# The first sum of a Laplacian stencil, computed by GpSimd instead of DVE, in a fused attention and convolution kernel

## The chip, the cores and the metric

One core of a Trainium2 chip runs the whole program. The metric is the time of one execution on the device in microseconds (us); several executions are timed, and the median counts. The engines are TensorE (PE, with its weight loads PEld), DVE (VectorE), ACT (ScalarE), POOL (GpSimd) and SP, which issues all DMAs here. They run in parallel, each through its own list of instructions, and meet at semaphores.

## The reference

The input x has the shape (8, 192, 128, 128), in float32. Two layers follow one another, each added to its input, each on a group-normalised input (`_gn`, 32 groups).

```python
x = x + _L0_conv_ref(_gn(x), ...)
x = x + _L1_conv_ref(_gn(x), merge_w, merge_b)
```

The first layer is attention within windows of 8x8 pixels with 6 heads of 32 channels. Queries and keys are multiplied in the frequency domain, the result meets the values, a position bias is added, then come softmax, the product with the values and a projection. The second layer is a Laplacian and a 1x1 convolution:

```python
lap = jnp.array([[0.0, -1.0, 0.0], [-1.0, 4.0, -1.0], [0.0, -1.0, 0.0]])
edges = lax.conv_general_dilated(x, lap_k, ..., feature_group_count=c)
out = x + edges
y = lax.conv_general_dilated(out, merge_w, window_strides=(1, 1), padding='VALID', ...)
```

So the second layer needs, for each pixel, five times itself minus its four neighbours: that is the stencil.

## The kernel before, in words

The work of the first layer is cut into 1024 pairs of windows (`PAIRS`), 128 per image. The kernel is one hand-written software pipeline: every engine runs the same loop over iterations `it`, and `pair(lag)` gives the pair whose step with that lag is due, so that six or so pairs are in flight. Eight iterations are a block (`blk, ph = divmod(it, 8)`), one strip of 8 image rows; 16 blocks are an image, and c is a block's number within its image. The second layer follows 17 blocks behind for the stencil (`STENCIL_LAG`) and 18 for the merge matmuls (`MERGE_LAG`). The order of work on each engine is the order in which the code of one iteration is written. Attention spans blocks 0 to 127, the stencil blocks 17 to 144, so blocks 17 to 127 have both.

One iteration, as far as the steps of the prediction touch it:

- TensorE transposes the probabilities (L418), runs one merge piece of the second layer (L394 to L401, phases 0 to 5), computes queries, keys and values (L456), transposes v (L460), projects (L472 to L475), multiplies probabilities and values (L485), transforms back (L495), transforms forward (L505), and forms the scores (L525).
- DVE adds the bias to the scores (L712), takes their maxima (L717), multiplies in the frequency domain (L721), finishes a merge piece (`result`, L697), runs the stencil and statistics steps that are due, splits q and k (`qkl`, L800, which L505 needs), adds the projection to x (L808), sums the exponentials (L818), splits part of x (L822), takes statistics (L705) and takes reciprocals (L851).
- GpSimd normalises the probabilities of one pair (L936, behind the reciprocal), splits x every fourth iteration (`xl`, L942, phases 2 and 6), and subtracts the maxima of a newer pair (L947, behind the maximum).
- ScalarE does the exponential (L904, behind L947) and then the copy `qkh` (called at L908, all copies are recorded at L859), which L800 needs.

The stencil of a strip has three units (channels 0 to 127 in two halves of four rows, and the 64 others). For each unit DVE runs three instructions:

- `diagonal` (L658): dg = the pixel rows below, shifted left, plus the rows above, shifted right; 5 rows of 129 elements from the tiles `src_a` or `src_b` (all parts of the tensor `late`);
- `neighbours` (L666): two shifted parts of dg are added, which gives the sum of the four neighbours;
- `stencil` (L674): 5 times the pixel minus that sum; phase 6 of the last unit lets the merge matmuls of the next block start.

`diagonal` is due in phases 0, 2 and 4, `neighbours` in 1, 3 and 5, `stencil` in 2, 4 and 6. dg has two buffers that the units use in turn. The first unit waits for the borders of the tile (`border_w`, written by DVE in phase 7) and for its load (`src_in`).

Other DVE steps stand behind the stencil in some blocks: the statistics of the next image's input (`stat_read`, L558, in phases 0, 1, 6 and 7 for c below 12, not in the last image); at c = 12 their aggregation (L564, phase 0); at c = 13 the scaled weights of the next image (L587 to L597, phases 2 to 4); at c = 1 the scaled merge weights (L794, phase 2).

Of the kernel before, what the change touches and what calls it, by code (L numbers as in the profile page):

```python
# [9 lines left out]
ALU = mybir.AluOpType  # L10
# [18 lines left out]
STENCIL_LAG, MERGE_LAG = 17, 18  # L29
# [61 lines left out]
def program(nc, x, out, w):  # L91
    B, _, H, W = x.shape
# [4 lines left out]
    PAIRS, STRIPS = B * NP, B * NS  # L97
# [7 lines left out]
    with ExitStack() as ctx:  # L105
        def sb(name, shape, dtype=F32):
            return ctx.enter_context(nc.sbuf_tensor(name, shape, dtype))
# [4 lines left out]
        def sem(name):  # L112
            return ctx.enter_context(nc.semaphore(name))
# [28 lines left out]
        dg = sb("dg", [128, 2, 5 * (W + 1)])  # L142
# [3 lines left out]
        src_a = [late[:, k * SA:(k + 1) * SA].rearrange("p (r c) -> p r c", c=PW) for k in range(3)]  # L146
        at = 3 * SA
        src_b = [late[:, at + k * SB:at + (k + 1) * SB].rearrange("p (r c) -> p r c", c=PW) for k in range(3)]
        at += 3 * SB
        za = late[:, at:at + 2048].rearrange("p (k n) -> p k n", k=2)  # L150
        zb = late[:, at + 2048:at + 3072].rearrange("p (k n) -> p k n", k=2)
# [21 lines left out]
        src_in = [sem(f"src_in{k}") for k in range(3)]  # L173
# [15 lines left out]
        border_w, diag_done, nb_done, z_done = map(sem, ("border_w", "diag_done", "nb_done", "z_done"))  # L189
# [39 lines left out]
        def pairs():  # L229

            def counted(i):
                return (i, i + 1) if 0 <= i < PAIRS else None
            for it in iterations:
                yield it, lambda lag, it=it: counted(it - lag)
# [11 lines left out]
        def tokens(o, t, h, up=0):  # L246
            lo = up
            return o[lo:lo + (CA if t == 0 else CB), h % 2, :].rearrange("p (w r c) -> p w r c", w=8, c=WS)

        block = ctx.enter_context(nc.Block())  # L250

# [279 lines left out]
        def _(dve):  # L531
            V = nc.vector
# [113 lines left out]
            def scored(i):  # L646
                return probs[:, i % 3, :, :]

            units = ((src_a, 0, za, 0), (src_b, 0, zb, 0), (src_a, 4, za, 512))

            def diagonal(v, unit):

                if unit == 0:
                    dve.wait_ge(border_w, v + 1)
                    dve.wait_ge(src_in[v % 3], 48 * (v // 3 + 1))
                src, r, _, _ = units[unit]
                s = src[v % 3]
                V.tensor_tensor(dg[:, unit % 2, :].rearrange("p (r c) -> p r c", c=W + 1),  # L658
                                s[:, r + 1:r + 6, 0:W + 1], s[:, r:r + 5, 1:W + 2], ALU.add).then_inc(diag_done, 1)

            def neighbours(v, unit):

                _, _, z, at = units[unit]
# [43 lines left out]
            for it, pair in pairs():  # L707
                blk, ph = divmod(it, 8)
# [18 lines left out]
                if task:  # L727
                    kind, at, p = task
# [24 lines left out]

                v = blk - STENCIL_LAG
                if 0 <= v < STRIPS:
                    if ph == 0:
                        diagonal(v, 0)
                    elif ph == 1:
                        neighbours(v, 0)
                    elif ph == 2:  # L760
                        stencil(v, 0)
                        diagonal(v, 1)
                    elif ph == 3:
                        neighbours(v, 1)
                    elif ph == 4:
                        stencil(v, 1)
                        diagonal(v, 2)
                    elif ph == 5:
                        neighbours(v, 2)
                    elif ph == 6:  # L770
                        stencil(v, 2)
                img, c = divmod(blk, NS)
# [72 lines left out]
                v = blk - STENCIL_LAG + 1  # L845
# [81 lines left out]
        @block.gpsimd  # L927
        def _(pool):
            P = nc.gpsimd
            P.memset(sm[:, :, :], 0.0)  # L930
            P.memset(ones[:, :], 1.0).then_inc(ones_done, 1)
            for it, pair in pairs():
                if pair(3):
                    i, n = pair(3)
                    pool.wait_ge(rec_done, n)
                    P.tensor_tensor(probs[:, i % 3, :, :], probs[:, i % 3, :, :],  # L936
                                    srec[:, i % 2, :].unsqueeze(2).broadcast_to([128, 6, N]),
                                    ALU.mult).then_inc(norm_done, 1)
                h = (it + 4) // 4
                if it % 4 == 2 and 0 <= h < PAIRS // 4:  # L940
                    pool.wait_ge(xh_done, 3 * h + 2)
                    P.tensor_tensor(tokens(xl, 0, h), windows(0, h), tokens(xh, 0, h).bitcast(F32), ALU.subtract  # L942
                                    ).then_inc(xl_done, 1)
                if pair(2):
                    i, n = pair(2)
                    pool.wait_ge(max_done, n)
                    P.tensor_tensor(probs[:, i % 3, :, :], probs[:, i % 3, :, :],  # L947
                                    smax[:, i % 2, :].unsqueeze(2).broadcast_to([128, 6, N]),
                                    ALU.subtract).then_inc(sub_done, 1)


# [28 lines left out]
```

## Time and profile before

| what | value |
|---|---|
| median of 3 runs | 6623.4 us (6617.2 to 6633.11) |
| profiled execution | 6616.41 us, span of its instructions 6614.6 us |
| TensorE busy | 6291.9 us (95%) |
| weight loads busy | 5340.6 us (81%) |
| DVE busy | 5312.2 us (80%), 11941 instructions |
| ScalarE busy | 3664.4 us (55%) |
| GpSimd busy | 2064.8 us (31%), 2310 instructions |
| mean granted clock of TensorE | 0.978 of full speed |

How to read it: busy time counts from the start to the end of each instruction; neighbouring instructions of one engine overlap a little, so a step in the chain can be shorter than the instruction itself. "Idle before" is the time in which an engine had nothing to do before an instruction, with the instruction that released it. The chain of work that ended last is followed back from the last instruction, at each step to what released it. Times in the trace are us from the start of the span.

### The profile page before, as it was taken

The page shows a single profiled execution, that of the slowest core. Times are in us where ns is not written, and L with a number is a line of the kernel's source. Part 1 is how long each engine was busy: PE and PEld are TensorE (multiplying, and loading weights), DVE is VectorE, ACT ScalarE, POOL GpSimd, SP SyncE. Part 2 cuts the span into 40 slices and gives each one's busy share as a digit, 9 for nine tenths or more (in the row PEclk, how much of TensorE's full clock was granted, in tenths as well). Part 3 has the DMA queues.
Part 4 walks back from the last instruction along what each step waited for, and adds up shares of the span by engine and source line. Part 5 has one row for each costly group of instructions (what it writes and reads, how often), then busy time and mean ns, then how long its engine had stood idle before and what let it go on. Part 6 is the DMA issues. An engine that isn't in the chain of part 4 may idle for free.

```text
span 6614.6 us, 222120 instructions
## 1 busy us (share of the span) xinstructions
PE 6291.9 (95%) x95620; PEld 5340.6 (81%) x95620; DVE 5312.2 (80%) x11941; ACT 3664.4 (55%) x9024; POOL 2064.8 (31%) x2310
## 2 busy tenths in 40 slices
PE   7999999999999999999999999999999999999976
PEld 5888788888888888888888888888888888888844
DVE  5777788888888888888888888888888888888854
ACT  3666655555555555555555555555555555555500
POOL 1333333333333333333333333333333333333300
PEclk9999999999999999999999999999999999999966
DMA  3221133232332322322333223323223222232233
GB/s 128 66 66 40 56 93 90 84 84 82 89 104 71 97 82 83 104 70 81 98 90 96 72 82 92 101 77 91 82 83 104 77 78 70 64 85 64 69 99 92
DMA packets 378995, 551.42 MB, mean 83 GB/s; under 512 B 23398, under 2 KB 283561, under 8 KB 365738
## 3 DMA queue, kind: packets, MB, share of 16 engines
q1 hardware_dynamic: 378028, 537.21, 28.5%
q8 instruction: 768, 12.58, 0.8%
q14 instruction: 199, 1.63, 0.1%
HBM read 335.80 MB, written 201.33 MB: 81 GB/s over the span
## 4 chain that ended last, share of the span: by engine, by line
PE 58%; DVE 25%; POOL 9%; ACT 6%; issue 2%; SPq 0%; DMA 0%; DVEq 0%; ACTq 0%
PE b_q L456 13%; PE b_t L505 7%; POOL probs L947 5%; PE b_s L525 5%; PE b_s L418 4%; DVE qkl L800 4%; DVE bn L705 4%; PE b_o L495 4%; PE b_o L394 3%; DVE late L808 3%; PE b_o L396 3%; ACT probs L904 3%; DVE ssum L818 3%; PE b_s L485 3%; POOL xl L942 3%; DVE probs L712 2%
## 5 line engine op out<-in xcount | busy, mean ns | idle before, releaser
L936 POOL TENSOR_TENSOR probs<-probs,srec 128x384 f32<-128x384 f32 x1024 | 849.3, 829 | 3723.1 <-DVE srec L851 3723.1
L800 DVE TENSOR_TENSOR qkl<-b_q,qkh 128x384 fp32r<-128x384 f32 x1024 | 567.6, 554 | 634.9 <-ACT qkh L859 628.3
L947 POOL TENSOR_TENSOR probs<-probs,smax 128x384 f32<-128x384 f32 x1024 | 908.0, 887 | 413.8 <-DVE smax L717 413.8
L712 DVE TENSOR_TENSOR probs<-b_s,posb 128x384 f32<-128x384 f32 x1024 | 553.0, 540 | 331.2 <-PE b_s L525 330.6
L904 ACT ACTIVATE probs<-probs 128x384 f32<-128x384 f32 x1024 | 535.3, 523 | 479.8 <-POOL probs L947 479.1
L456 PE MATMUL b_q<-wnh,xh 128*128 128x192 f32 (+1 forms) x2048 | 791.7, 387 | 3.1 <-DVE xhl L822 2.7
L859 ACT ACTIVATE probsT<-b_s 128x384 f32<-128x384 f32 x1024 | 502.4, 491 | 501.3 <-PE b_s L418 501.3
L859 ACT ACTIVATE qh<-b_t 94x384 f32<-94x384 f32 x1024 | 498.4, 487 | 480.4 <-PE b_t L505 480.4
L525 PEld LDWEIGHTS b_s<-vT,osb 32*64 32x64 f32 x24576 | 450.6, 132 | 284.5 <-ACT osb L859 204.9
L859 ACT ACTIVATE yT<-b_s 128x256 f32<-128x256 f32 x1024 | 392.7, 384 | 460.3 <-PE b_s L485 458.2
L456 PE MATMUL b_q<-wnl,xh 128*128 128x192 f32 (+1 forms) x2048 | 632.5, 309 | 0.0
L808 DVE SCALAR_TENSOR_TENSOR late<-b_s,pb,xs 128x128 f32<-128x128 f32 (+1 forms) x2048 | 610.1, 339 | 27.2 <-PE b_s L475 5.2
L456 PE MATMUL b_q<-wnl,xhl 128*128 128x192 f32 (+1 forms) x2048 | 631.0, 308 | 0.0
L456 PE MATMUL b_q<-wnh,xhb 128*128 128x192 f32 (+1 forms) x2048 | 630.5, 308 | 0.0
L456 PE MATMUL b_q<-wnh,xl 128*128 128x192 f32 (+1 forms) x2048 | 629.6, 307 | 0.0
L859 ACT ACTIVATE vs<-b_q 128x192 f32<-128x192 f32 x1024 | 334.9, 327 | 518.6 <-PE b_q L456 512.9
L717 DVE TENSOR_REDUCE smax<-probs 128x6 f32<-128x384 f32 x1024 | 566.5, 553 | 35.5
L525 PE MATMUL b_s<-vT,osb 32*64 32x64 f32 x24576 | 592.4, 225 | 0.9 <-DVE late L808 0.7
L505 PE MATMUL b_t<-qkh,fwdh 64*94 64x384 f32 x2048 | 423.1, 410 | 171.0 <-DVE qkl L800 170.7
L495 PE MATMUL b_o<-inv_sb,prod 94*64 94x64 f32 x12288 | 582.9, 230 | 0.0
L418 PE MATMUL b_s<-ident_sb,probs 128*128 128x128 f32 x3072 | 561.3, 292 | 1.2 <-ACT yT L859 1.2
L721 DVE TENSOR_TENSOR prod<-qh,b_t 94x384 f32<-94x384 f32 x1024 | 553.5, 541 | 1.9 <-ACT qh L859 1.9
(143 smaller groups left out, 15231.2 us busy)
## 6 DMA issues: line engine op xcount, KB each, us to landing
ld<-in_x SPq DMA_DIRECT2D x96, 1024.0 KB, 4.9
late<-x_dram SPq DMA_DIRECT2D x112, 640.0 KB, 6.3
xs<-in_x SPq DMA_DIRECT2D x128, 512.0 KB, 5.7
x_dram<-late SPq DMA_DIRECT2D x128, 512.0 KB, 2.8
out<-late SPq DMA_DIRECT2D x128, 512.0 KB, 4.6
late<-x_dram SPq DMA_DIRECT2D x240, 192.0 KB, 6.7
xs<-in_x SPq DMA_DIRECT2D x128, 256.0 KB, 6.3
x_dram<-late SPq DMA_DIRECT2D x128, 256.0 KB, 3.6
```

What stands on the lines that cost most here:

```text
L418: last = nc.tensor.transpose(b_p[:, t * 128:(t + 1) * 128], probs[:, i % 3, 2 * t:2 * t + 2, :].rearrange("p w m -> p (w m)"), ident[:, :])
L456: last = mm(o, xx[:, h % 2, at], ww[:, par, t, lo:up], start=(k == 0), stop=(k == 4))
L495: last = mm(b_o[g * N:(g + 1) * N, k * N:(k + 1) * N], prod[:, g * 3 + k, :, :].rearrange("p h d -> p (h d)"), inv[:, :], start=True, stop ...
L505: last = mm(b_t[0:NF, win * 512:win * 512 + QK], ff[rows, :], xx[rows, :], start=(k == 0), stop=(k == 2))
L525: last = mm(scores[h * N:(h + 1) * N, s * N:(s + 1) * N], osb[r:r + HD, k, :], vT[r:r + HD, i % 2, int(t > g), win * N:(win + 1) * N], sta ...
L712: V.tensor_tensor(scored(i).rearrange("p (t w) m -> p t w m", w=2), scores.rearrange("p (t w m) -> p t w m", w=2, m=N), posb[:, :, :].unsq ...
L800: V.tensor_tensor(qkl[:, :], q_out, qkh[:, :].bitcast(F32), ALU.subtract).then_inc(lo_out, 1)
L808: last = V.scalar_tensor_tensor(out=x1s[0:m, t, u % 2, :].rearrange("p (r c) -> p r c", c=W)[:, :, col:col + 16], in0=b_r[0:m, t * 128:(t ...
L859: return A.activation(o, i, ACT.Copy)
L904: A.activation(pr, pr, ACT.Exp).then_inc(exp_done, 1)
L936: P.tensor_tensor(probs[:, i % 3, :, :], probs[:, i % 3, :, :], srec[:, i % 2, :].unsqueeze(2).broadcast_to([128, 6, N]), ALU.mult).then_i ...
L947: P.tensor_tensor(probs[:, i % 3, :, :], probs[:, i % 3, :, :], smax[:, i % 2, :].unsqueeze(2).broadcast_to([128, 6, N]), ALU.subtract).th ...
```

## The change

`diagonal` goes from DVE's list to GpSimd's, at the end of GpSimd's iteration, behind the subtraction of the maxima, in the same phases 0, 2 and 4. On GpSimd it waits, beside the borders and the load, for `nb_done`, so that the dg buffer it writes has been read. The operands, the shape and the two buffers are the same. `neighbours` and `stencil` stay on DVE and wait for `diag_done` as before.

```diff
@@ -646,18 +648,6 @@
-            def diagonal(v, unit):
-
-                if unit == 0:
-                    dve.wait_ge(border_w, v + 1)
-                    dve.wait_ge(src_in[v % 3], 48 * (v // 3 + 1))
-                src, r, _, _ = units[unit]
-                s = src[v % 3]
-                V.tensor_tensor(dg[:, unit % 2, :].rearrange("p (r c) -> p r c", c=W + 1),
-                                s[:, r + 1:r + 6, 0:W + 1], s[:, r:r + 5, 1:W + 2], ALU.add).then_inc(diag_done, 1)
...
@@ -753,18 +743,14 @@
-                    if ph == 0:
-                        diagonal(v, 0)
-                    elif ph == 1:
+                    if ph == 1:
                         neighbours(v, 0)
                     elif ph == 2:
                         stencil(v, 0)
-                        diagonal(v, 1)
                     elif ph == 3:
                         neighbours(v, 1)
                     elif ph == 4:
                         stencil(v, 1)
-                        diagonal(v, 2)
...
@@ -929,7 +915,20 @@
+            def diagonal(v, unit):
+                if unit == 0:
+                    pool.wait_ge(border_w, v + 1)
+                    pool.wait_ge(src_in[v % 3], 48 * (v // 3 + 1))
+                if 3 * v + unit >= 2:
+                    pool.wait_ge(nb_done, 3 * v + unit - 1)
+                src, r, _, _ = units[unit]
+                s = src[v % 3]
+                P.tensor_tensor(dg[:, unit % 2, :].rearrange("p (r c) -> p r c", c=W + 1),
+                                s[:, r + 1:r + 6, 0:W + 1], s[:, r:r + 5, 1:W + 2], ALU.add).then_inc(diag_done, 1)
+
             for it, pair in pairs():
+                blk, ph = divmod(it, 8)
...
@@ -947,6 +946,9 @@
+                v = blk - STENCIL_LAG
+                if 0 <= v < STRIPS and ph in (0, 2, 4):
+                    diagonal(v, ph // 2)
```

DVE's list in phase 0 of an ordinary block, before (from the scores' bias to the split of q and k; the waits stand in brackets):

```order
L712 TENSOR_TENSOR probs<-b_s,posb 128x384 [waits s_mm]
L717 TENSOR_REDUCE smax<-probs 128x6 [waits s_out]
L721 TENSOR_TENSOR prod<-qh,b_t 94x2x3x64 [waits qh_out]
L697 SCALAR_TENSOR_TENSOR late<-b_o,mc,late 128x256 [waits out_sent0,m_mm]
L658 TENSOR_TENSOR dg<-late 128x645 [waits src_in0,border_w]
L558 BN_STATS bn<-ld 128x6 [waits ld_in1]
L800 TENSOR_TENSOR qkl<-b_q,qkh 128x384 [waits hi_out]
```

And the same place now (the changed file's lines are shifted: L702 is the old L712, L786 the old L800):

```order
L702 TENSOR_TENSOR probs<-b_s,posb 128x384 [waits s_mm]
L707 TENSOR_REDUCE smax<-probs 128x6 [waits s_out]
L711 TENSOR_TENSOR prod<-qh,b_t 94x2x3x64 [waits qh_out]
L687 SCALAR_TENSOR_TENSOR late<-b_o,mc,late 128x256 [waits out_sent0,m_mm]
L560 BN_STATS bn<-ld 128x6 [waits ld_in1]
L786 TENSOR_TENSOR qkl<-b_q,qkh 128x384 [waits hi_out]
```

The addition and its two waits are gone from between `result` and the statistics; nothing else has moved on DVE.

GpSimd's list before, over three iterations, the last of them with the split of x:

```order
L936 TENSOR_TENSOR probs<-probs,srec 128x384 [waits rec_done]
L947 TENSOR_TENSOR probs<-probs,smax 128x384 [waits max_done]
L936 TENSOR_TENSOR probs<-probs,srec 128x384 [waits rec_done]
L947 TENSOR_TENSOR probs<-probs,smax 128x384 [waits max_done]
L936 TENSOR_TENSOR probs<-probs,srec 128x384 [waits rec_done]
L942 TENSOR_TENSOR xl<-xs,xh 128x512 [waits xh_done]
L947 TENSOR_TENSOR probs<-probs,smax 128x384 [waits max_done]
```

And now, phases 0, 1 and 2 of a block (L935, L941 and L946 are the old L936, L942 and L947; the addition is listed under L927, the head of GpSimd's part):

```order
L935 TENSOR_TENSOR probs<-probs,srec 128x384 [waits rec_done]
L946 TENSOR_TENSOR probs<-probs,smax 128x384 [waits max_done]
L927 TENSOR_TENSOR dg<-late 128x645 [waits nb_done,src_in2,border_w]
L935 TENSOR_TENSOR probs<-probs,srec 128x384 [waits rec_done]
L946 TENSOR_TENSOR probs<-probs,smax 128x384 [waits max_done]
L935 TENSOR_TENSOR probs<-probs,srec 128x384 [waits rec_done]
L941 TENSOR_TENSOR xl<-xs,xh 128x512 [waits xh_done]
L946 TENSOR_TENSOR probs<-probs,smax 128x384 [waits max_done]
L927 TENSOR_TENSOR dg<-late 128x645 [waits nb_done]
```

The addition stands behind the subtraction and in front of the next iteration's normalisation, which waits for DVE's reciprocal.

## Rows read from the trace of the kernel before

**Rows 1.** The page: busy time of the engines; the chain that ended last, by engine

```profile
PE 6291.9 (95%) x95620; PEld 5340.6 (81%) x95620; DVE 5312.2 (80%) x11941; ACT 3664.4 (55%) x9024; POOL 2064.8 (31%) x2310
...
PE 58%; DVE 25%; POOL 9%; ACT 6%; issue 2%; SPq 0%; DMA 0%; DVEq 0%; ACTq 0%
```

**Rows 2.** Groups of instructions: names, shapes xcount | busy us, mean ns | idle before us

```profile
L936 POOL TENSOR_TENSOR probs<-probs,srec 128x384 f32<-128x384 f32 x1024 | 849.3, 829 | 3723.1 <-DVE srec L851 3723.1
...
L942 POOL TENSOR_TENSOR xl<-xs,xh 128x512 fp32r<-128x512 f32 x256 | 328.4, 1283 | 102.2 <-ACT xh L859 102.2
...
L658 DVE TENSOR_TENSOR dg<-late 128x645 f32<-128x645 f32 x384 | 315.8, 822 | 0.0
```

**Rows 3.** The chain in order of time, phases 5 to 0: start us, us, what

```profile
2657.38 0.60 DVE late L808 x2
...
2661.29 1.25 POOL probs L947
...
2675.66 0.76 PE b_t L505 x6
```

**Rows 4.** The chain, L658 in phase 0: first, second and last of 65

```profile
906.27 0.74 DVE dg L658
...
954.46 0.74 DVE dg L658
...
5276.56 0.74 DVE dg L658
```

**Rows 5.** Timeline, phase 0 of an ordinary block: start us, us, engine, instruction [idle before]

```profile
2674.32 0.47 ACT L859 ACTIVATE qkh<-b_q 128x384 fp32r<-128x384 f32 x1
2674.47 0.68 DVE L558 BATCH_NORM_STATS2 bn<-ld 128x6 f32<-128x512 f32 x1
...
2675.07 0.53 DVE L800 TENSOR_TENSOR qkl<-b_q,qkh 128x384 fp32r<-128x384 f32 x1
...
2675.66 0.41 PE L505 MATMUL b_t<-qkh,fwdh 64*94 64x384 f32 x2 [0.43 <-DVE qkl L800]
```

**Rows 6.** Timeline, phase 0 of a block of the last image

```profile
6011.23 0.56 DVE L800 TENSOR_TENSOR qkl<-b_q,qkh 128x384 fp32r<-128x384 f32 x1 [0.28 <-ACT qkh L859]
```

**Rows 7.** Timeline of TensorE: c = 12 in phase 0, c = 13 in phases 2 and 4

```profile
2965.55 0.42 PE L505 MATMUL b_t<-qkh,fwdh 64*94 64x384 f32 x2 [1.12 <-DVE qkl L800]
...
3026.34 0.42 PE L505 MATMUL b_t<-qkh,fwdh 64*94 64x384 f32 x2 [0.33 <-DVE qkl L800]
...
3039.64 0.41 PE L505 MATMUL b_t<-qkh,fwdh 64*94 64x384 f32 x2 [0.91 <-DVE qkl L800]
```

**Rows 8.** Timelines of GpSimd and TensorE, c = 1, phase 2

```profile
2440.69 2.77 POOL L947 TENSOR_TENSOR probs<-probs,smax 128x384 f32<-128x384 f32 x1
...
2445.04 0.55 PE L505 MATMUL b_t<-qkh,fwdh 64*94 64x384 f32 x2 [1.59 <-DVE qkl L800]
```

**Rows 9.** Timelines of GpSimd, DVE and TensorE: phase 0, then phase 2, then phase 4

```profile
2673.03 0.83 POOL L947 TENSOR_TENSOR probs<-probs,smax 128x384 f32<-128x384 f32 x1 [0.19 <-DVE smax L717]
2676.88 0.83 POOL L936 TENSOR_TENSOR probs<-probs,srec 128x384 f32<-128x384 f32 x1 [3.02 <-DVE srec L851]
...
2636.04 0.84 POOL L947 TENSOR_TENSOR probs<-probs,smax 128x384 f32<-128x384 f32 x1
2639.97 0.83 POOL L936 TENSOR_TENSOR probs<-probs,srec 128x384 f32<-128x384 f32 x1 [3.09 <-DVE srec L851]
...
2636.67 0.76 DVE L674 SCALAR_TENSOR_TENSOR late<-late 128x512 f32<-128x512 f32 x1
...
2638.09 0.55 DVE L800 TENSOR_TENSOR qkl<-b_q,qkh 128x384 fp32r<-128x384 f32 x1
...
2639.35 0.41 PE L505 MATMUL b_t<-qkh,fwdh 64*94 64x384 f32 x2
...
2648.95 0.68 DVE L674 SCALAR_TENSOR_TENSOR late<-late 128x512 f32<-128x512 f32 x1
```

**Rows 10.** The last 304 us: busy PE, PEld, DVE, ACT, POOL; clock, DMA share, GB/s

```profile
6310.00:6614.00 304.00, 212.51 (x517) 130.15 (x515) 159.83 (x313) 0.64 (x2) 0.00 (x0) 0.63 0.38 101
```

More of the change, by code:

```diff
@@ L248, in tokens @@
             return o[lo:lo + (CA if t == 0 else CB), h % 2, :].rearrange("p (w r c) -> p w r c", w=8, c=WS)
+        units = ((src_a, 0, za, 0), (src_b, 0, zb, 0), (src_a, 4, za, 512))
         block = ctx.enter_context(nc.Block())
@@ L647, in scored @@
                 return probs[:, i % 3, :, :]
-            units = ((src_a, 0, za, 0), (src_b, 0, zb, 0), (src_a, 4, za, 512))
-            def diagonal(v, unit):
-                if unit == 0:
-                    dve.wait_ge(border_w, v + 1)
-                    dve.wait_ge(src_in[v % 3], 48 * (v // 3 + 1))
-                src, r, _, _ = units[unit]
-                s = src[v % 3]
-                V.tensor_tensor(dg[:, unit % 2, :].rearrange("p (r c) -> p r c", c=W + 1),
-                                s[:, r + 1:r + 6, 0:W + 1], s[:, r:r + 5, 1:W + 2], ALU.add).then_inc(diag_done, 1)
             def neighbours(v, unit):
```

## The prediction

> **What bounds the kernel now.** I read the page first. TensorE is busy 95% of the span, DVE 80%, GpSimd 31%; the chain of work that ended last lies 58% on TensorE, 25% on DVE and 9% on GpSimd [rows 1]. So TensorE sets the pace most of the time, and DVE, GpSimd and ScalarE set it in detours. What counts is where in the chain the moved instruction stands, not the 315.8 us that it keeps DVE busy.
>
> The list of instruction groups gives the moved work: 384 additions of 128x645 (L658) at 822 ns each on DVE. It also shows GpSimd's idle time: 3723.1 us before its 1024 normalisations, 3.6 us per iteration [rows 2].
>
> The chain, read in order of time for an ordinary block of eight iterations (48.2 us, from one L658 of rows 4 to the next), is TensorE alone from phase 0 to phase 5. It then leaves TensorE for some 18 us: from L808 in phase 5 over the softmax steps of phases 6 and 7 on GpSimd, ScalarE and DVE, to L658 in phase 0, L558 and L800, and back to TensorE at L505 [rows 3]. So of the three L658 in a block only that of phase 0 is on the chain. Those of phases 2 and 4 run while TensorE has work of its own. That pattern stands 65 times in the chain, from 906.27 to 5276.56 us [rows 4]: where c, a block's number within its image, is 2 to 11 in six images, and 0 in five of them. The image borders (c = 12, 13 and 1) are priced apart.
>
> **What the change removes and adds.** DVE loses 384 x 0.822 = 315.8 us. A step of 0.74 us goes out of the chain wherever L658 stood there, because neighbouring DVE instructions overlap by 0.08 us. GpSimd gains 384 additions behind the max-subtraction of the same iteration. No copy of dg and no DMA is added, and SP's queue is not touched. The two waits of unit 0 (border_w and src_in) go from DVE's queue to GpSimd's; queued behind them there is the next normalisation. Both signals were there when DVE came to them: no idle time stands before L658 [rows 2].
>
> *Price of one addition on GpSimd.* No row has this shape. 829 ns for 384 elements [rows 2] gives 829/384 x 645 = 1.39 us; 1283 ns for 512 [rows 2] gives 1.62; a straight line through both gives 1.75. I take 1.39, because L942 reads short windows of 8 while the addition reads runs of 129, and keep 1.75 as the upper end. The Trainium skill, GPSIMD Engine Reference, section 3 (its table for tensor_tensor), states 4497 ns for 2048 fp32 elements; an estimate from it would be 1.42 us, and the page advises VectorE for element-wise work. By that advice the change would lose; by the rows the slower engine has the room for it, and with 1.42 the sum would stay as it is.
>
> *What hides it.* In phase 0 the subtraction ends at 2673.86 and the next normalisation starts at 2676.88: 3.02 us of room for 1.39. In phase 2 it ends at 2636.88 and the next starts at 2639.97: 3.09 us, of which DVE's L674 may take 0.55 first [rows 9]. So the additions cost nothing on GpSimd. If one took over 2.5 us it would push the softmax chain. Its consumer, the second sum L666, is in the next iteration, some 5 us later, so the new semaphore is early.
>
> *Ordinary blocks, phase 0.* Without L658, L558 ends before the ScalarE copy of qkh does (2674.32 + 0.47 = 2674.79). L800 then starts at about 2674.82 instead of 2675.07: 0.25 us, and the rest of the 0.74 turns into a wait for qkh [rows 5]. Next late is thus subtraction, exponential, qkh. Image 7 is a natural check: it has no L558, and there L800 waits 0.28 us for qkh although L658 is still in front [rows 6]. TensorE sat idle 0.43 us before L505 [rows 5], so it takes the whole 0.25. 65 x 0.25 = **16.3 us**. Ends: 0 and 65 x 0.43 = 28.
>
> *c = 12, phase 0.* In place of L558 a longer aggregation follows (L564), and TensorE idles 1.12 us [rows 7]: the whole step counts. 6 x 0.74 = **4.4 us**.
>
> *c = 13, phases 2 and 4.* The weights of the next image are made on DVE behind L658. TensorE idles 0.33 us in phase 2 and 0.91 in phase 4 [rows 7]. The first 0.33 comes back and starts the next phases earlier; the 0.74 of phase 4 comes on top. 6 x 1.07 = **6.4 us**. Ends: 6 x 0.33 = 2 and 6 x 1.24 = 7.4.
>
> *c = 1, phase 2.* Here the subtraction takes 2.77 us instead of 0.83 and TensorE idles 1.59 us [rows 8]. It lies behind L674, L658 and the scaling L794 of DVE, which keep GpSimd waiting one after the other. Taking L658 out gives 0.74 back. Five of the six blocks look like this, and I price the sixth the same: 6 x 0.74 = **4.4 us**. Ends: 0, if GpSimd loses the same time elsewhere, and 4.9. The Trainium skill, SBUF — State Buffer, section "Who interferes with whom", says that a VectorE instruction with two SBUF inputs and a GpSimd one that reads SBUF shut each other out for a whole instruction; by that rule the 2.77 is as read here, and the same rule can turn against the change (below).
>
> *The end*, 304 us after the last attention pair: TensorE's granted clock is 0.63 there, a mix of its two levels, 1.2 and 2.4 GHz, and DVE is busy only 159.8 us [rows 10]. The merge matmuls alternate with L697 and L658 runs beside them. I put it at 0; ends -10 to +10, for a clock that falls otherwise.
>
> Phases 2 and 4 of ordinary blocks: nothing, since TensorE covers them. In phase 2 L505 starts 0.71 us after L800 has ended (2639.35 against 2638.64) [rows 9].
>
> **Sum.** 16.3 + 4.4 + 6.4 + 4.4 = 31.5 us. The profiled execution took 6616.4 us, so it would take 6585. The median of the three runs shown is 7.0 us above it, 6623.4; on that footing **6592 us**, 0.5% faster. A measurement of this kernel can tell about 0.2%, 13 us, from no change.
>
> **Rivals.**
> 1. *Every microsecond of L658 in the chain counts*: the chain has 65 + 6 + 6 common places of 0.74 us, 57 us; with the 4.4 of c = 1 and some 6 us of pieces at the borders and in the end that is 67 us: 6556. For: softmax and DVE steps might shift together. Against: the wait for qkh in rows 6, with less in front of L800. 0.07.
> 2. *The phase 0 gain is taken by the next wait*: only the image borders pay, 4 to 16 us: about 6613. For: the margin is only 0.25 us, and an addition on GpSimd may slow something there. Against: the ScalarE path has no L658 in it. 0.13.
> 3. *Slower: GpSimd's addition gets in front of DVE's stencil (L674) in phase 2.* Behind the subtraction both want to start; today L674 starts 0.2 us before the subtraction ends and takes 0.76 us, where in phase 4 it takes 0.68 [rows 9]. If the addition came first, from 2636.88 to 2638.27, L674 would follow with its 0.68, 0.08 of them overlapped, and L800 would start at 2638.87 instead of 2638.09: 0.78 late against a slack of 0.71. That costs 0.07 x 111 blocks (as many have both attention and stencil) = 8 us, and 6600 remains a gain. It turns to a loss of over 13 us once the addition takes over 1.72 us: (31.5 + 13) / 111 = 0.40 per block, 0.33 more than that 0.07. At the upper end of 1.75 it costs 0.43 x 111 = 48 us: 6640. Against: in phase 6 DVE's L674, not the GpSimd subtraction queued behind another GpSimd instruction, went first, and the subtraction took 1.25 us for it [rows 3]. By the rule of the Trainium skill cited above, SBUF — State Buffer, the one that starts first holds on, which leaves the order open here. 0.03 for slower, 0.05 for the milder form at 6600.
> 4. *No change*: DVE's shorter work is swallowed everywhere, 6623. Against: rows 7, where TensorE plainly waits for DVE. 0.04.
>
> **How the numbers follow.** My forecast, a gain of 22 to 45 us, has 0.68; rivals 0.07, 0.13, 0.08 and 0.04. The range leaves out the extremes of rivals 1, 3 and 4, takes in most of rival 2 and the unknown ends (28 for 16.3, the clock of the end, runs that lie 6 below and 10 above their median): 6568 to 6612. Faster by over 0.2% holds the forecast, rival 1, the milder form of rival 3 and half of rival 2: 0.87. Within 0.2%: the rest of rival 2 and rival 4, 0.10. Slower: 0.03.
>
> **What would show it.** GpSimd's busy time rises by about 535 us (384 x 1.39), DVE's falls by 316. The addition stands nowhere in the chain; L800 in phase 0 of ordinary blocks shows a wait for qkh of about 0.4 us, and TensorE's idle before L505 falls from 0.43 to about 0.2. The subtraction in c = 1 takes about 2.0 us. It is wrong if the addition takes over 1.7 us, if L674 in phase 2 gets longer than 0.76 us, if the next normalisation waits behind the addition, or if a block stays at 48.2 us.

## The result, and the profile after

| | before | after |
|---|---|---|
| median of 12 runs each | 6625.7 us (6611.7 to 6643.8) | 6610.1 us (6605.4 to 6617.0) |
| profiled execution | 6616.4 us | 6612.3 us |
| span of its instructions | 6614.6 us | 6610.5 us |

The ratio is 0.9977 with a 95% interval of 0.9967 to 0.9986: 15.6 us faster, just past the 0.2% that a measurement can tell, and half of the 31.5 us that were forecast. The sign was right and the size was not. The median lies inside the stated range of 6568 to 6612 us, by 2 us.

The page after the change, busy time and the chain by engine, answering to [rows 1]:

```profile
PE 6300.0 (95%) x95620; PEld 5341.1 (81%) x95620; DVE 5076.1 (77%) x11557; ACT 3662.7 (55%) x9024; POOL 2738.8 (41%) x2694
...
PE 58%; DVE 22%; POOL 11%; ACT 7%; issue 2%; SPq 0%; DMA 0%; POOLq 0%; DVEq 0%; ACTq 0%
```

DVE's share of the chain fell from 25 to 22%, GpSimd's rose from 9 to 11%. The addition itself stands nowhere in the chain, as forecast. GpSimd's share rose because in phase 0 the chain now comes over its normalisation and its subtraction to the exponential and qkh. GpSimd is busy 674 us longer (535 forecast), DVE 236 us shorter (316 forecast). The groups of GpSimd, with the same columns as [rows 2]:

```profile
L935 POOL TENSOR_TENSOR probs<-probs,srec 128x384 f32<-128x384 f32 x1024 | 849.2, 829 | 3112.0 <-DVE srec L837 3112.0
...
L927 POOL TENSOR_TENSOR dg<-late 128x645 f32<-128x645 f32 x384 | 692.7, 1806 | 209.8 <-DVE late L673 154.1
```

The addition takes 1.81 us in the mean. The timeline says why. These are first phase 0 of an ordinary block, then phase 2 of the same block (start us, us, engine, instruction, idle before), all engines:

```profile
2618.20 0.83 POOL L946 TENSOR_TENSOR probs<-probs,smax 128x384 f32<-128x384 f32 x1 [0.19 <-DVE smax L707]
2618.99 1.57 POOL L927 TENSOR_TENSOR dg<-late 128x645 f32<-128x645 f32 x1
2620.00 0.56 DVE L786 TENSOR_TENSOR qkl<-b_q,qkh 128x384 fp32r<-128x384 f32 x1 [0.42 <-ACT qkh L845]
2620.61 0.41 PE L507 MATMUL b_t<-qkh,fwdh 64*94 64x384 f32 x2 [0.19 <-DVE qkl L786]
2621.82 0.83 POOL L935 TENSOR_TENSOR probs<-probs,srec 128x384 f32<-128x384 f32 x1 [1.27 <-DVE srec L837]
...
2629.83 0.75 DVE L664 SCALAR_TENSOR_TENSOR late<-late 128x512 f32<-128x512 f32 x1
2629.99 2.01 POOL L927 TENSOR_TENSOR dg<-late 128x645 f32<-128x645 f32 x1
```

Undisturbed, an addition takes 1.57 us: dearer than the 1.39 taken, inside the bounds. In phase 2 it stands 0.44 us longer, issued while DVE's stencil (L664, the old L674) runs. That costs nothing: the next normalisation still waits for its reciprocal, 1.27 us in phase 0 and 1.13 us in phase 2. Phase 0 went as forecast: L786 (the old L800) now waits 0.42 us for qkh, and TensorE's idle time before L507 (the old L505) fell from 0.43 [rows 5] to 0.19.

An ordinary block now takes 48.0 us instead of 48.2. I measured each block in both traces, from its L800 (now L786) in phase 0 to the next one's. Over images 1 to 6, the difference sorts like this (minus is faster; each row counts what its term was forecast for):

| place | forecast | measured |
|---|---|---|
| phase 0 of 65 ordinary blocks | -16.3 | -13.4 (0.21 each) |
| c = 12, phase 0, six | -4.4 | -4.2 |
| c = 13, six | -6.4 | **+8.6** |
| c = 1, six | -4.4 | -5.8 |
| c = 0 and the rest | 0 | +1.1 |
| images 1 to 6 | -31.5 | -13.7 |

Of the shortfall of 17.8 us, 15.0 us are one row: at c = 13 the sign is wrong. Behind the last L800 the program ran 322.0 us in the profiled execution of before and 331.6 in that of after, which is why these two differ by only 4.1 us; the experiments take that up.

The timeline of DVE and GpSimd at c = 13, phases 2 and 4 of image 3, shows the loss. The two rows of the weights, L589 and L598, are the old L587 and L596:

```profile
3014.43 0.84 DVE L664 SCALAR_TENSOR_TENSOR late<-late 128x512 f32<-128x512 f32 x1
3014.68 2.01 POOL L927 TENSOR_TENSOR dg<-late 128x645 f32<-128x645 f32 x1
3015.19 2.24 DVE L589 TENSOR_SCALAR wn<-wq,cst 128x576 f32<-128x576 f32 x2
...
3028.10 0.69 DVE L664 SCALAR_TENSOR_TENSOR late<-late 128x512 f32<-128x512 f32 x1
3028.20 2.00 POOL L927 TENSOR_TENSOR dg<-late 128x645 f32<-128x645 f32 x1
3028.71 2.11 DVE L598 TENSOR_TENSOR wnl<-wn,wnh 128x576 fp32r<-128x576 f32 x1
```

The same two steps in the trace of before:

```profile
3024.75 0.94 DVE L587 TENSOR_SCALAR wn<-wq,cst 128x576 f32<-128x576 f32 x2
...
3037.71 0.75 DVE L596 TENSOR_TENSOR wnl<-wn,wnh 128x576 fp32r<-128x576 f32 x1
```

GpSimd's addition is issued while the stencil runs and waits. Between the end of the stencil and the weight step behind it, it gets in, and now DVE's weight step is longer by 1.30 us in phase 2 (2.24 against 0.94) and by 1.36 in phase 4 (2.11 against 0.75), the same in all six images. The chain of waits after the change runs through it (start us, us, what):

```profile
3028.18 0.60 DVE late L664
3028.79 2.03 DVE wnl L598
3030.82 0.67 DVE wnl L599
3031.49 0.48 DVE qkl L786
```

The timeline of TensorE in phase 4, image 3 and then image 4:

```profile
3032.01 0.41 PE L507 MATMUL b_t<-qkh,fwdh 64*94 64x384 f32 x2 [1.53 <-DVE qkl L786]
...
3033.21 0.55 PE L420 MATMUL b_s<-ident_sb,probs 128*128 128x128 f32 x3
...
3816.41 0.44 PE L507 MATMUL b_t<-qkh,fwdh 64*94 64x384 f32 x2 [1.51 <-DVE qkl L786]
...
3818.26 0.90 PE L420 MATMUL b_s<-ident_sb,probs 128*128 128x128 f32 x3
```

TensorE idles 1.53 us where it had idled 0.91 [rows 7]. In image 4 something comes on top: the same three transposes (L420) take 0.90 us instead of 0.55. The windows of 5 us from the same point show it (the columns are those of [rows 10]):

```profile
3031.40:3036.40 5.00, 4.39 (x50) 3.85 (x51) 4.59 (x13) 2.24 (x5) 1.66 (x2) 1.00 0.62 185
3815.80:3820.80 5.00, 4.39 (x40) 3.50 (x40) 3.29 (x9) 1.49 (x3) 1.66 (x2) 0.66 0.62 179
```

The granted clock is 1.00 in image 3 and 0.66, a mix of 2.4 and 1.2 GHz, in image 4, right behind the long idle time. From L800 in phase 4 to that of phase 5, image 3 takes 5.63 us and image 4 takes 7.15: here one such fall costs 1.52 us.

### The profile page after: what moved, and what is told of

Same layout as the page of the kernel before. It is cut to its first block, busy times and chain, and to the rows that moved or that the text cites. A ratio compares the mean times of both kernels' runs of the same rounds, so it can differ in the third digit from the quotient of the medians.

```text
span 6610.5 us, 222120 instructions
## 1 busy us (share of the span) xinstructions
PE 6300.0 (95%) x95620; PEld 5341.1 (81%) x95620; DVE 5076.1 (77%) x11557; ACT 3662.7 (55%) x9024; POOL 2738.8 (41%) x2694
## 4 chain that ended last, share of the span: by engine, by line
PE 58%; DVE 22%; POOL 11%; ACT 7%; issue 2%; SPq 0%; DMA 0%; POOLq 0%; DVEq 0%; ACTq 0%
PE b_q L458 13%; PE b_t L507 7%; POOL probs L946 6%; PE b_s L527 5%; PE b_s L420 4%; DVE qkl L786 4%; DVE bn L695 4%; PE b_o L497 3%; ACT probs L890 3%; PE b_o L396 3%; DVE late L794 3%; PE b_o L398 3%; POOL probs L935 3%; DVE ssum L804 3%; POOL xl L941 3%; PE b_s L487 3%
## 5 line engine op out<-in xcount | busy, mean ns | idle before, releaser
L935 POOL TENSOR_TENSOR probs<-probs,srec 128x384 f32<-128x384 f32 x1024 | 849.2, 829 | 3112.0 <-DVE srec L837 3112.0
L786 DVE TENSOR_TENSOR qkl<-b_q,qkh 128x384 fp32r<-128x384 f32 x1024 | 570.6, 557 | 821.2 <-ACT qkh L845 815.2
L946 POOL TENSOR_TENSOR probs<-probs,smax 128x384 f32<-128x384 f32 x1024 | 902.4, 881 | 413.7 <-DVE smax L707 413.7
L702 DVE TENSOR_TENSOR probs<-b_s,posb 128x384 f32<-128x384 f32 x1024 | 553.1, 540 | 329.8 <-PE b_s L527 328.9
L927 POOL TENSOR_TENSOR dg<-late 128x645 f32<-128x645 f32 x384 | 692.7, 1806 | 209.8 <-DVE late L673 154.1
L527 PEld LDWEIGHTS b_s<-vT,osb 32*64 32x64 f32 x24576 | 450.4, 132 | 284.9 <-ACT osb L845 204.2
L794 DVE SCALAR_TENSOR_TENSOR late<-b_s,pb,xs 128x128 f32<-128x128 f32 (+1 forms) x2048 | 610.4, 340 | 31.7 <-PE b_s L477 7.0
L527 PE MATMUL b_s<-vT,osb 32*64 32x64 f32 x24576 | 592.3, 225 | 0.5 <-ACT osb L845 0.4
L507 PE MATMUL b_t<-qkh,fwdh 64*94 64x384 f32 x2048 | 423.2, 410 | 158.5 <-DVE qkl L786 157.7
L420 PE MATMUL b_s<-ident_sb,probs 128*128 128x128 f32 x3072 | 560.9, 292 | 1.2 <-ACT yT L845 1.2
```

The costliest lines, as they stand in the source:

```text
L420: last = nc.tensor.transpose(b_p[:, t * 128:(t + 1) * 128], probs[:, i % 3, 2 * t:2 * t + 2, :].rearrange("p w m -> p (w m)"), ident[:, :])
L507: last = mm(b_t[0:NF, win * 512:win * 512 + QK], ff[rows, :], xx[rows, :], start=(k == 0), stop=(k == 2))
L527: last = mm(scores[h * N:(h + 1) * N, s * N:(s + 1) * N], osb[r:r + HD, k, :], vT[r:r + HD, i % 2, int(t > g), win * N:(win + 1) * N], sta ...
L786: V.tensor_tensor(qkl[:, :], q_out, qkh[:, :].bitcast(F32), ALU.subtract).then_inc(lo_out, 1)
L794: last = V.scalar_tensor_tensor(out=x1s[0:m, t, u % 2, :].rearrange("p (r c) -> p r c", c=W)[:, :, col:col + 16], in0=b_r[0:m, t * 128:(t ...
L927: P.tensor_tensor(dg[:, unit % 2, :].rearrange("p (r c) -> p r c", c=W + 1), s[:, r + 1:r + 6, 0:W + 1], s[:, r:r + 5, 1:W + 2], ALU.add). ...
```

## The experiments

All medians are compared with runs of the kernel before on the same chip. The expectations name the readings by letters. A is the one of the section above: the forecast was right but for c = 13, where the addition holds DVE's weight steps. D is that the length of the end goes with TensorE's clock and not with the kernel. The other letters are their rivals, told there. What was measured per place is a sum over images 1 to 6 as above, of one profiled execution against the first profile of the kernel before; for c = 1 it is the whole block, with phase 0 of c = 2 in it, which the table counts in its first row.

**e1_no_sum: what is it worth to take the first sum off DVE?** The first sum is left out altogether: dg is filled with zeros once, and the stencil's later steps run on it. The edit is against the kernel before: `diagonal` keeps only the waits of its first unit, and `neighbours` no longer waits for the sum.

```diff
-                V.tensor_tensor(dg[:, unit % 2, :].rearrange("p (r c) -> p r c", c=W + 1),
-                                s[:, r + 1:r + 6, 0:W + 1], s[:, r:r + 5, 1:W + 2], ALU.add).then_inc(diag_done, 1)
...
-                dve.wait_ge(diag_done, 3 * v + unit + 1)
...
+            P.memset(dg[:, :, :], 0.0)
```

> This is the kernel before with the first sum left out altogether: dg is filled with zeros once, the waits for borders and loads stay on DVE; the stencil's output is computed from zeros. Theory A (what the change gives back, it loses where GpSimd's addition keeps the shared way into SBUF from the weight instructions of c = 13): without an addition anywhere the forecast gain is there in full: ordinary blocks 48.0 us, c = 11/12 border 0.7 us less, c = 13 about 1.0 us below the kernel before (48.4 instead of 49.4 us), c = 1 about 0.7 to 1.4 us less; in all 28 to 34 us, ratio about 0.9953. Theory B (DVE's time is simply not worth more, other waits take over): c = 13 gains nothing and the ratio is about 0.9975, as for the change. Theory C (the end of the program got longer through the change): the last L800 to the end takes 322 us here, as in the kernel before.

Measured: 6598.0 us against 6617.0, ratio 0.9971 (0.9959 to 0.9982). Per place: ordinary blocks 0.22 each, c = 12 -4.4, c = 13 -6.3, images 1 to 6 -33.0. So the forecast of 31.5 us was nearly the worth of a stencil without its first sum. The medians are only 19 us apart, and the ratio that A gave is missed. In the profiled execution the rest is in the end, which took 343.1 us, 21 more than before, though no addition runs there at all. So C is not borne out. This execution was the longest of its six (6607.3 us), so how much of the gap between the medians the end explains is not shown.

**e2_c13_on_dve: only the two additions of c = 13 go back to DVE.**

```diff
                     elif ph == 2:
                         stencil(v, 0)
+                        if blk % NS == 13:
+                            diagonal(v, 1)
...
                     elif ph == 4:
                         stencil(v, 1)
+                        if blk % NS == 13:
+                            diagonal(v, 2)
...
-                if 0 <= v < STRIPS and ph in (0, 2, 4):
+                if 0 <= v < STRIPS and ph in (0, 2, 4) and (ph == 0 or not (blk % NS == 13)):
```

> The change, but in blocks with c = 13 the sums of units 1 and 2 stay on DVE. Theory A: c = 13 goes back from 50.5 to the 49.4 us of the kernel before, in all 6 x 1.2 to 1.5 us = 7 to 9 us less than the change; ratio 0.9960 to 0.9967. Theory B: c = 13 unchanged at 50.5 us, ratio 0.9977. Theory C: the end takes about 330 us as in the change, since it has the same code there.

Measured: 6599.6 us against 6617.0, ratio 0.9971 (0.9959 to 0.9982). c = 13 is back at the 49.4 us of before (+0.06 in the sum), and the ordinary blocks stay as in the change. A single c = 12 took 3.1 us longer, where TensorE's clock fell behind an idle time of 1.49 us. 12 of 384 additions carry 8.6 us. The medians alone could not have told this: the ratio misses the 0.9960 to 0.9967 that A gave, and its interval covers the change's 0.9977.

**e3_c13_wait: the additions of c = 13 stay on GpSimd, but start behind DVE's split of q and k.** One wait is added in two phases of one block in 16:

```diff
                 if 0 <= v < STRIPS and ph in (0, 2, 4):
+                    if blk % NS == 13 and ph and pair(0):
+                        pool.wait_ge(lo_out, pair(0)[1])
                     diagonal(v, ph // 2)
```

> The change, but in phases 2 and 4 of c = 13 GpSimd waits for lo_out of the iteration (DVE's L800) before it starts the addition, so that DVE's weight instructions come first. Theory A: the weight instructions take 0.94 and 0.75 us again, c = 13 falls below the kernel before, to 48.3 to 48.5 us; 6 x 2.2 = 13 us less than the change, ratio about 0.9955 to 0.9960. Theory B: the later addition pushes the next normalisation and c = 13 stays at or above 50.5 us. Theory C: the end as in the change, 330 us.

Measured: 6587.4 us against 6617.0, ratio 0.9960 (0.9947 to 0.9973). At c = 13, five of six images gain 1.10 to 1.16 us each; the other loses 1.35. There, in a single phase 7, TensorE stood 1.57 us amid the matmuls of L527, with no cause that the profile shows, and its clock fell behind it; this did not come again in the repeat below.

**e4_unit0_only: only the additions of phase 0 on GpSimd**, those of phases 2 and 4 on DVE as before.

```diff
                     elif ph == 2:
                         stencil(v, 0)
+                        if True:
+                            diagonal(v, 1)
...
                     elif ph == 4:
                         stencil(v, 1)
+                        if True:
+                            diagonal(v, 2)
...
-                if 0 <= v < STRIPS and ph in (0, 2, 4):
+                if 0 <= v < STRIPS and ph in (0, 2, 4) and (ph == 0 or not (True)):
```

> Only unit 0 (phase 0) goes to GpSimd, units 1 and 2 stay on DVE everywhere. Theory A: ordinary blocks 48.0 us (65 x 0.2 = 13 us) and 4 us at c = 12, nothing at c = 13 and c = 1 (49.4 us and the 2.8 us subtraction stay): 17 to 18 us, ratio about 0.9973; about as fast as the change although only a third of the work is moved. Theory B: the ordinary blocks share the gain of all three units and reach only 48.1 us, ratio 0.999. Theory C: with DVE's units 1 and 2 back at the end, it takes about 322 us as in the kernel before.

Measured: 6596.6 us against 6617.0, ratio 0.9965 (0.9951 to 0.9978). A third of the moved work gives as much as all of it, in this profile more: -25.1 us over images 1 to 6, c = 13 at +0.1. The miss is c = 1, where A expected nothing and 6.1 us were gained. Phase 0 of c = 2 lies in that sum with 6 x 0.25 = 1.5. Then TensorE's clock: behind the 1.59 us of idle time [rows 8] it fell in two images of before, as the window from that point shows, for 1.53 us each, and once in phase 4, for 0.33. Here it fell at none of these places, though TensorE idled 1.59 us in two images here too.

```profile
2444.40:2449.40 5.00, 4.36 (x41) 3.49 (x42) 3.48 (x9) 1.74 (x5) 1.66 (x2) 0.66 0.00 0
```

The third part is GpSimd's subtraction in phase 2. In two images it got in ahead of the scaling L794 here, and not before. This is GpSimd's timeline in one of them, here and then before:

```profile
1650.01 2.11 POOL L959 TENSOR_TENSOR probs<-probs,smax 128x384 f32<-128x384 f32 x1
```

```profile
1653.68 2.78 POOL L947 TENSOR_TENSOR probs<-probs,smax 128x384 f32<-128x384 f32 x1
```

That is worth 0.66 us each. 1.5 + 3.4 + 1.3 = 6.2. The last two parts differ between images of one and the same kernel too, so whether the moved phase 0 has a hand in them is not shown.

**e5_before_again and e6_after_again: both kernels once more, on another chip.**

> The kernel before, unchanged, for a second profile and for what a ratio of a kernel to itself looks like. Theory C (the change makes the end of the program longer): the time from the last L800 to the end is 322 us again, within 3 us, with a share of slow merge matmuls there of 0.63. Theory D (the clock of the end falls differently in each execution, whatever the kernel): it lies anywhere between 320 and 343 us. Ratio 1.000 with an interval of about 0.001 to each side by both.

> The changed kernel, unchanged. Ratio 0.9977 again, within 0.001. The attention part (first to last L800) is 13 to 15 us shorter than in the first profile of the kernel before. Theory C: the end takes 330 to 333 us again. Theory D: anywhere between 320 and 343 us.

Measured: the kernel before gives 6625.2 us against 6622.7 (ratio 1.0002, 0.9992 to 1.0012), the change 6611.1 against 6622.7 (0.9976, 0.9966 to 0.9986). c = 13 repeats at +8.8 us, with the fall of the clock in image 4 again. The profile of e5 against the first profile of the same kernel shows what the sums per place are worth: 0.0 us in the ordinary blocks, 0.2 at c = 12 and at c = 13, but +3.4 at c = 1 and +4.9 in all, with four falls of the clock where the first profile had three. So the row of c = 13 stands clear of this scatter and that of c = 1 does not. The end took 331.4 us in the kernel before itself and 328.4 in the change. The windows of the last 304 us, of after, of the kernel before again, and of e1_no_sum, beside the 0.63 of [rows 10]:

```profile
6306.50:6610.50 304.00, 217.48 (x494) 131.60 (x494) 119.52 (x250) 0.20 (x1) 73.69 (x48) 0.59 0.35 94
```

```profile
6323.30:6627.30 304.00, 217.53 (x495) 131.77 (x494) 152.25 (x299) 0.20 (x1) 0.00 (x0) 0.59 0.36 95
```

```profile
6301.60:6605.60 304.00, 218.68 (x474) 131.27 (x472) 111.14 (x229) 0.00 (x0) 0.00 (x0) 0.56 0.35 92
```

The granted clock orders the ends: 0.63 with 322.0 us, 0.59 with 331.6 and 331.4, 0.56 with 343.1, whether the additions run there on DVE, on GpSimd or not at all. The other profiles fall into the same order: 0.62 with 325.0 and 325.4 (e2, e10), 0.60 with 328.4 and 329.6 (e6, e9), 0.59 with 332.4 and 332.3 (e3, e8), 0.57 with 338.4 and 340.0 (e4, e7). The kernel before alone gave 322.0 and 331.4. This is D, so far as it goes: with one or two profiles of each kernel, a difference of a few us between kernels is not excluded.

**e7_wait_end_dve: as e3, and in the end the additions back on DVE.** **e8_c13_wait_again: e3 once more.**

```diff
+                    if ph == 0 and blk >= PAIRS // 8:
+                        diagonal(v, 0)
...
-                if 0 <= v < STRIPS and ph in (0, 2, 4):
+                if 0 <= v < STRIPS and ph in (0, 2, 4) and blk < PAIRS // 8:
```

> The change with the wait on lo_out in c = 13, and with all three sums back on DVE in the blocks behind the attention (block 128 and later). Theory C: the end takes 322 us as in the kernel before and the ratio is 0.9950 to 0.9960, some 10 us below the variant with GpSimd at the end. Theory D: the end lies anywhere between 320 and 343 us, and the ratio is that of the variant with the wait alone.

> The change with the wait on lo_out in c = 13 a second time, beside the variant with the end on DVE. Both theories: the attention part is 26 us shorter than that of the kernel before, or some 31 us where no single iteration is disturbed. Theory C: the end 332 us again and the ratio 0.9965. Theory D: the end anywhere between 320 and 343 us, the ratio between 0.9955 and 0.9965, and the time 12 to 16 us below the change's in the same call.

Measured: 6594.9 us (0.9958, 0.9945 to 0.9970) and 6596.1 us (0.9957, 0.9945 to 0.9969), against 6622.7: the same. In e7 the end took 340.0 us, with its additions on DVE, where C expected 322. So the additions in the end cost nothing that can be seen. In e8, c = 13 gives -6.9 us, the term as it was forecast (-6.4), and images 1 to 6 give -32.9, as much as without the sum at all. The timeline of DVE, then of TensorE, in phase 4 of c = 13 there:

```profile
3022.24 0.75 DVE L598 TENSOR_TENSOR wnl<-wn,wnh 128x576 fp32r<-128x576 f32 x1
```

```profile
3024.17 0.41 PE L507 MATMUL b_t<-qkh,fwdh 64*94 64x384 f32 x2 [0.16 <-DVE qkl L786]
```

**e9_c13_c1_wait: the same wait also in phase 4 of c = 1.** There, after the change, the addition got ahead of the stencil itself, which took 1.99 us instead of 0.68. Timeline of DVE and GpSimd after the change:

```profile
2449.86 1.58 POOL L927 TENSOR_TENSOR dg<-late 128x645 f32<-128x645 f32 x1
2449.99 1.99 DVE L664 SCALAR_TENSOR_TENSOR late<-late 128x512 f32<-128x512 f32 x1
```

> The change with the wait on lo_out in c = 13 (phases 2 and 4) and also in phase 4 of c = 1, where the stencil of unit 1 (L674 of the kernel before) takes 1.99 us instead of 0.68 behind GpSimd's addition. Theory A (an addition on GpSimd costs what it holds up on DVE, wherever DVE is on the chain): the stencil takes 0.68 us again in all blocks with c = 1, those blocks get 0.4 to 0.6 us shorter, 7 x 0.55 = 4 us less than with the wait in c = 13 alone; attention part 36 us shorter than in the first profile of the kernel before, ratio 0.9950 to 0.9955. Rival: DVE has slack in c = 1, phase 4, and the blocks stay at 49.0 us; ratio 0.9957 as before.

Measured: 6594.2 us against 6617.2, ratio 0.9961 (0.9948 to 0.9973). The stencil is back at its length, and c = 1 stays at -7.5 us (-7.6 in e8): the rival was right. The timeline of DVE says why:

```profile
2442.32 0.68 DVE L664 SCALAR_TENSOR_TENSOR late<-late 128x512 f32<-128x512 f32 x1
...
2443.88 0.56 DVE L786 TENSOR_TENSOR qkl<-b_q,qkh 128x384 fp32r<-128x384 f32 x1 [0.87 <-ACT qkh L845]
```

With no hold DVE waits 0.87 us for qkh. A hold of 1.31 us made L786 at most 0.4 us later (by image), and the next phase took that back. At c = 13 no such room stands behind L598: L599 and L786 follow without idle time.

**e10_c13_wait_ph2: the wait in phase 2 of c = 13 alone.**

```diff
-                    if blk % NS == 13 and ph and pair(0):
+                    if blk % NS == 13 and ph == 2 and pair(0):
```

> The change with the wait on lo_out in phase 2 of c = 13 alone; in phase 4 the addition still comes first. Theory A: the first scaling of the weights takes 0.51 us again, the first remainder (L598) still 2.11; each of the two holds costs about half of the 2.35 us per image: c = 13 at 49.2 to 49.5 us, 7 us less than the change, ratio 0.9965 to 0.9970. Rival (the two holds are not additive, since the next iteration waits for whichever is later): c = 13 stays at 50.5 us, or falls at once to 48.3 us.

Measured: 6610.3 us against 6617.2, ratio 0.9986 (0.9977 to 0.9995): half of the holds are gone, and the gain does not come halfway. c = 13 reads +7.5 us, two images at +0.2 and four at +1.8. Phase 2 is free and phase 4 is held, as DVE's timeline shows:

```profile
3012.52 0.94 DVE L589 TENSOR_SCALAR wn<-wq,cst 128x576 f32<-128x576 f32 x2
...
3025.06 2.11 DVE L598 TENSOR_TENSOR wnl<-wn,wnh 128x576 fp32r<-128x576 f32 x1
```

A expected half of the loss back and missed; its rival, that c = 13 stays or falls back at once, missed too. The windows of TensorE behind phase 4, in an image at +0.2 and in one at +1.8, show why:

```profile
2244.20:2249.20 5.00, 4.34 (x50) 3.79 (x51) 4.59 (x13) 2.22 (x5) 1.66 (x2) 1.00 0.61 178
3027.70:3032.70 5.00, 4.34 (x40) 3.54 (x40) 3.34 (x9) 1.50 (x3) 1.66 (x2) 0.66 0.61 178
```

In four images the clock fell behind an idle time of 1.52 to 1.54 us, where it had fallen in one after the change. With both parts the sums close. e10 stands 14.4 us above e8 at c = 13; the hold of phase 4 makes L786 1.37 us later (25.86 against 24.49 us from the block's start), 6 x 1.37 = 8.2, and four falls add some 6.2. The change stands 15.5 above e8; both holds make L786 of phase 4 later by 26.82 - 24.49 = 2.33, 6 x 2.33 = 14.0, and one fall adds 1.5. Why the clock falls behind one idle time of 1.5 us and not behind the next is open.

The waiting form beats both kernels, by 23 to 30 us against the one before (e3, e8, e9), where the change gives 12 to 16. On one chip all five runs of e8 (6593.2 to 6597.3 us) lie below all eight of the change (e6, 6602.2 to 6615.3), and the medians differ by the 15 us that c = 13 was short.

## Why the prediction was right and wrong

**Right: which work is on the chain.** Of three L658 in a block only that of phase 0 counts; e4 shows it, with a third of the moved work and the whole gain of the ordinary blocks (0.21 us each). The cap by qkh (0.25 forecast, 0.21 measured), c = 12 (4.4 and 4.2) and the sum itself held: without the hold at c = 13, images 1 to 6 give 32.9 us against 31.5.

**Wrong: the term for c = 13, and with it the statement that the additions cost nothing.** I wrote "6 x 1.07 = 6.4 us" from DVE's side alone. Its weight steps stand in line behind the stencil, without idle time, and TensorE waits for them: exactly there a GpSimd instruction that comes at the same moment costs time. Taking L658 away even moved the weight steps to where the addition is issued. The term came out as a loss of 8.6 us, of which 1.5 are one fall of TensorE's clock, and as a gain of 6.9 once the addition waits.

**Right mechanism, wrong place: rival 3.** It asked whether the addition gets ahead of L674 in phase 2 of all 111 blocks, and there it didn't: L664 took 0.75 us, against 0.76 before. I never asked what stands behind L674. Its argument was weak as well. I took from one subtraction of 1.25 us [rows 3] and one of 2.77 [rows 8] that DVE's instructions in line keep GpSimd out. The same trace held the contrary, in three rows of DVE's timeline:

```profile
690.25 1.38 DVE L597 TENSOR_TENSOR wnl<-wn,wnh 64x576 fp32r<-64x576 f32 x1
...
868.47 1.45 DVE L658 TENSOR_TENSOR dg<-late 128x645 f32<-128x645 f32 x1
...
3230.45 0.98 DVE L794 TENSOR_SCALAR mn<-wm,sm 128x384 f32<-128x384 f32 x1
```

In all other images before, L597 takes 0.74 us, L658 0.82 and this L794 0.41; in these places a subtraction of GpSimd got in between two DVE instructions that follow each other. The second row is the moved instruction itself, behind the stencil, in the first block with c = 1. The rule of the Trainium skill that I cited, SBUF — State Buffer, section "Who interferes with whom", agrees with what came, 2.11 us for L598 and 2.01 for the addition: one shuts the other out until it has ended, both ways. The runs show only which of the two stood while the other worked, not the path that they share. I used the rule for GpSimd's wait in c = 1 and not for DVE's at c = 13.

**Mis-sized, without effect.** The addition takes 1.57 us, not 1.39, and 2.01 where it waits. Its mean of 1.81 is above the 1.7 that I had named as a sign of being wrong; the sign was badly chosen, since L664 in phase 2 kept its length and no normalisation waited. GpSimd's busy time rose by 674 us, and none of it reached the chain in ordinary blocks. DVE's busy time fell by 236 us, not 316, since the additions had overlapped their neighbours by 0.08 us each (31 us) and since the held instructions count as busy while they stand (some 37 us; the last 12 are open).

**c = 1: the size nearly, the reason only half.** The subtraction there went from 2.77 to 2.04 us, as forecast (2.0). I had counted five of six blocks with 2.77; the trace of before has four, one with 2.10 and one with 1.28. And of the 5.8 us measured, some 2.6 come from TensorE's clock, which fell three times around c = 1 before (1.53, 1.53 and 0.33 us) and once after (0.81). That leaves 3.2 us for the 4.4 of the term, so that the total came near it is partly luck. A term for the clock was missing from the attention part altogether; at c = 1 and c = 13 a fall cost between 0.3 and 1.6 us, by its place.

**The end** was put at 0 with 10 us to either side; the profiles show 322 to 343 us, and for the unchanged kernel 322 and 331.

**The range was luck.** It reached to 6612 for other reasons, most of rival 2 and the unknown ends. None of them is a GpSimd addition that holds DVE's weight steps.

## What to carry to other kernels

Before an instruction goes from DVE to GpSimd, look not only at the room on the new engine but at what the old engine has in line at that very moment. Where DVE's steps are on the chain without idle time, the moved instruction can cost nearly its own length there (1.3 of 1.57 us here), even if nobody waits for its result. Such places were few here (12 of 384) and sat at the borders where extra steps are due; one wait that puts the moved instruction behind the step that the chain needs took the loss away. And read the idle time of TensorE twice, once for itself and once for the clock that may fall behind it.

## What was not expected of the hardware

- An instruction of GpSimd that is already waiting gets in between two DVE instructions that follow each other: before L589 and L598 in every image. At other places it depends on the block. In phase 2 of c = 1 GpSimd's subtraction stood through three DVE instructions in four of six images of before (2.77 us), got in ahead of the third in one (2.10) and ahead of the second in one (1.28). What decides it there was not found.
- A held instruction counts as busy: the page shows DVE at work while it stands, and no idle time gives the hold away. Only the length of one instruction against its own kind does.
- TensorE's clock falls in the middle of the attention part. It does so in every image but the first, in every kernel, around phase 5 of c = 0, where the engine idles 3.16 to 3.52 us; the row of TensorE's timeline and the window from there show it in one image of before. Elsewhere it falls behind single idle times of 1.5 to 1.7 us, in some images and not in others: in images 1 to 6, 3 times before and 4 in its repeat e5, twice after and once in its repeat e6, 4 times in e10, twice in e3 and in e7 (there once with no idle time above 0.94 us just before), once in e2, not at all in e1, e4, e8 and e9. At c = 13 the three transposes that follow take 0.90 us instead of 0.55.

```profile
2410.48 0.35 PE L377 MATMUL b_o<-sm,mates_sb 128*128 128x2 f32 x2 [3.16 <-DVE sm L833]
```

```profile
2410.00:2415.00 5.00, 4.52 (x19) 4.40 (x20) 4.45 (x11) 0.74 (x2) 2.84 (x3) 0.60 0.53 70
```

- The end of the program differs by up to 21 us between executions, with the clock granted there (0.63 to 0.56).
